# First layer's experts by slots: routed tiles of 128 rows in place of all eight experts over every row

## The reference, cut to what matters

```
x = x + tanh(g_xattn[0]) * _L0_xattn_ref(ctx_2048, _layernorm(x, axis=-1), L0_xattn_b, itok)
x = x + tanh(g_ffn[0]) * _L0_ffn_ref(_layernorm(x, axis=-1), W_qkv, b_qkv, W_gate, b_gate, W_experts, b_experts)
...
def _L0_ffn_ref(x, ...):                       # E = 8 experts, D = 256, TOP_K = 2, 16 heads of 16
    ...                                        # self-attention: attn_out
    gate = jax.nn.softmax(x @ W_gate + b_gate, axis=-1)
    top_g, top_i = jax.lax.top_k(gate, TOP_K)
    combine = jnp.sum(jax.nn.one_hot(top_i, E, dtype=x.dtype) * top_g[..., None], axis=2)
    expert_out = jnp.einsum('bsd,edf->bsef', x, W_experts) + b_experts
    moe_out = jnp.einsum('bsef,bse->bsf', expert_out, combine)
    return attn_out + moe_out
```

## Time and profile before

| | |
|---|---|
| Time, median of 3 runs | 2596.88 us (2596.45 to 2602.02) |
| The profiled execution | 2595.37 us, its span 2593.6 us |
| Busy share of the span | PE 88%, PEld 61%, DVE 64%, ACT 52%, POOL 39% |
| Unit 0's jobs | to about 385 us of the span |
| Unit 1's jobs (with the dense experts) | about 385 to 985 us |
| Units 2 and 3 | about 985 to 1520, and to 1890 us |
| Routing, second layer's experts, their sum | about 1890 to 2594 us |

### The profile page before, as it was taken

One profiled execution on the slowest core, in us unless ns is written; L12 is line 12 of the kernel. 1 busy time (PEld: TensorE's weight loads), 2 busy tenths in 40 slices (PEclk: granted clock), 3 DMA queues, 4 the chain that ended last, 5 costly groups with the idle time before them and its releaser, 6 DMA issues. The chain is left out here.

```text
span 2593.6 us, 51898 instructions
## 1 busy us (share of the span) xinstructions
PE 2280.5 (88%) x17492; PEld 1577.5 (61%) x17493; DVE 1658.5 (64%) x4377; ACT 1358.8 (52%) x2398; POOL 1004.2 (39%) x1875
## 2 busy tenths in 40 slices
PE   2889999899999999999999999999837999999950
PEld 1444555555455556666666666766527999999950
DVE  4878886677766667777767777786644434343437
ACT  3889863555336456777777788776601222222212
POOL 5556412213022135333323347887611333333323
PEclk9999998999999999999999999999956999999985
DMA  7878623314134245555555445555264111111125
GB/s 219 208 187 205 159 72 82 76 46 114 44 90 96 64 98 134 123 119 121 127 129 123 119 103 123 137 125 131 54 217 147 34 36 34 36 35 34 36 84 194
DMA packets 212014, 279.68 MB, mean 108 GB/s; under 512 B 32734, under 2 KB 156617, under 8 KB 205546
## 3 DMA queue, kind: packets, MB, share of 16 engines
q1 hardware_dynamic: 198378, 246.57, 38.5%
q0 software_dynamic: 6912, 17.97, 2.2%
q10 hardware_dynamic: 6528, 12.58, 1.3%
HBM read 193.12 MB, written 84.83 MB: 107 GB/s over the span
## 5 line engine op out<-in xcount | busy, mean ns | idle before, releaser
L1012 ACT ACTIVATE ex<-t_ps 128x512 f32<-128x512 f32 (+1 forms) x1280 | 684.9, 579 | 200.8 <-PE t_ps L918 153.8
L1163 DVE TENSOR_REDUCE mx<-s_ps 128x2 f32<-128x512 f32 (+1 forms) x1024 | 660.0, 683 | 198.4 <-PE s_ps L889 123.8
L918 PE MATMUL t_ps<-qs,ks 123*128 123x256 bf16 x2048 | 354.8, 276 | 9.6 <-ACT ex L1012 4.6
L941 PE MATMUL pv_ps<-ex,va 128*17 128x256 f32 (+1 forms) x5120 | 318.3, 375 | 0.7 <-POOL ex L1064 0.5
L1006 ACT ACTIVATE qs<-tr_ps 27x2048 bf16<-27x2048 bf16 x128 | 239.2, 1869 | 107.8 <-PE tr_ps L902 104.9
L918 PEld LDWEIGHTS t_ps<-qs,ks 123*128 123x128 bf16 x2048 | 176.4, 98 | 156.2 <-ACT ex L1012 68.3
L1571 PEld LDWEIGHTS x_up_ps<-x_rows_t,x_wnow 128*128 128x128 f32 x2272 | 267.3, 193 | 5.3 <-issue 0.9
L859 PE MATMUL pre_ps<-wexp,xt 128*128 128x512 f32 x512 | 266.3, 625 | 3.7 <-DVE moe L1225 2.7
L1571 PE MATMUL x_up_ps<-x_rows_t,x_wnow 128*128 128x128 f32 x2272 | 267.9, 277 | 1.1 <-ACT x_rows_t L1601 1.1
L1601 ACT ACTIVATE x_rows_t<-x_rt_ps 128x256 f32<-128x256 f32 x72 | 27.6, 383 | 448.5 <-PE x_rt_ps L1560 448.5
L1581 PE MATMUL x_y_ps<-wdn,x_act 128*128 x1136 | 257.1, 379 | 0.7 <-DVE x_y L1642 0.7
(11 more groups left out here) (244 smaller groups left out, 3741.4 us busy)
## 6 DMA issues: line engine op xcount, KB each, us to landing
q_parts<-pq SPq DMA_DIRECT2D x128, 192.0 KB
qs<-q_parts SPq DMA_DIRECT2D x64, 384.0 KB, 4.9
qs<-q_parts SPq DMA_DIRECT2D x192, 128.0 KB, 5.8
k_parts<-pk SPq DMA_DIRECT2D x96, 192.0 KB
ks<-k_parts SPq DMA_DIRECT2D x96, 192.0 KB
ks<-k_parts SPq DMA_DIRECT2D x288, 64.0 KB
ks<-ctx_k_parts SPq DMA_DIRECT2D x64, 192.0 KB
ks<-ctx_k_parts SPq DMA_DIRECT2D x192, 64.0 KB
```

The source lines that it names most:

```text
L918: last = pe.matmul(dst[:, t * T:(t + 1) * T], key[0:ROWS, h, t * P:(t + 1) * P], qs[q_at][0:ROWS, h, :], start=True, stop=True)
L941: last = pe.matmul(pv_ps[i * VS:i * VS + VW, q0:T], val[:, t, k * QH + i, :], e, start=r == 0 and t == 0, stop=r == srcs - 1 and t == NT - ...
L1012: act.activation(ex[:, n % EXPS, 0:w], t_ps[n % 2][:, 0:w], ACT.Exp).then_inc(t_read, 1)
L1163: dve.tensor_reduce(dst, s_ps[n % S_BANKS][:, :].rearrange("p (a b) -> p a b", a=dst.shape[-1]), AX.X, ALU.max).then_inc(s_read, 1)
```

## The change

The dense steps (`GATE`, `GEXP`, `TOP`, `CT`, `MBIAS`, `EXPERT`) and `moe` go. Instead:

- **Unit 0's jobs**, after `FIN`, also do the norm for unit 1: `HNS` (DVE), `HNP` (POOL), `HNX` (DVE, into `o`), store it (`STOREN`, 256 KB), turn it (`HT`: PE, ACT) and compute the gate's logits (`HG`: PE, DVE).
- **Unit 1's jobs** load that norm (`LOADN`) straight into `xn` in place of `LNS`, `LNP`, `LNX`.
- **The routing** of all 4096 rows is one chain, begun when the last `HG` of unit 0 is done: 23 steps `RC` on DVE, one `RX` on ACT, `RANK` on PE, then 16 chunks `RH` (DVE), `TH` (DVE, POOL), `NAME` (PE, DVE). It stands in the order between the first two jobs of unit 1.
- **71 tiles** of 128 rows, eight to each job (1, 2) to (1, 10): `XR` (POOL: indirect gather into one of 6 buffers), `XTT` (PE reads the tile's expert into a register and turns the rows; ACT copies), `XE` (PE: bias by a bf16 matmul and two f32 matmuls of 256 columns; DVE copies), `XS` (POOL: indirect scatter from one of 4 buffers). All 71 are done whatever the rows' experts are.
- **Unit 2's jobs** load the two rows per token (`LOADY`, 512 KB) and add them to x (`MOE`, four multiply-adds on DVE) before `LNS`. `LOADY` of the first job waits for all scatters.
- The second layer's `w1` and `wo` lie in the space of `wexp` and are loaded behind `LOADX` of job (3, 0), no longer at the start; the experts' bias is loaded three times at the start, behind the large weights, and cut into bf16 parts there by 10 DVE operations.

```
-    "GATE": [("pe", 0.9), ("dve", 0.65)], "GEXP": [("act", 0.22)], "TOP": [("dve", 0.6)],
-    "CT": [("pe", 0.25), ("act", 0.36)], "MBIAS": [("pe", 1.1), ("dve", 0.69)], "EXPERT": [("pe", 0.87), ("pe", 0.87), ("dve", 0.97)],
...
+def tile_job(n):
+    return 1, 2 + n // 8
...
-    s = add("LNS", 0, x, past("LNX", 2))
-    s = add("LNX", 0, add("LNP", 0, s), past("XT", 2) if u < 3 else None)
+    if u == 1:
+        s = add("LOADN", 0, ("STOREN", 0, b, 0), past("XT", 2))
+    else:
+        if u == 2:
+            y = add("LOADY", 0, *([("MOE", u, b - 2, 0)] if b >= 2 else [("XS", *tile_job(n), n) for n in range(SLOT_TILES)]))
+            x = add("MOE", 0, x, y)
+        s = add("LNS", 0, x, past("LNX", 2, 0, (0, 2, 3)))
+        s = add("LNX", 0, add("LNP", 0, s), past("XT", 2) if u < 3 else None)
...
-    if u == 1:
-        chain = add("GEXP", 0, add("GATE", 0, turned, ("FIN", u, b - 2, 0) if b >= 2 else None))
-        for n in range(TOPS):
-            chain = add("TOP", n, chain)
-        chain = add("MBIAS", 0, add("CT", 0, chain))
-        experts = [add("EXPERT", (t, e), chain) for t in range(NT) for e in range(0, E, 2)]
...
+    if u in (0, 3):
+        s = add("HNX", 0, add("HNP", 0, add("HNS", 0, s, ("HNX", u, b - 2, 0) if b >= 2 else None)))
+        if u == 0:
+            add("STOREN", 0, s)
+            s = add("HT", 0, s, past("HG", NQ))
...
+def expert_steps():
...
+    add(rc(0), *[("HG", 0, b, 0) for b in range(B)])
+    add(("RX", 1, 0, 0), rc(0))
+    for k in range(1, CHAIN):
+        after = {1: ("RX", 1, 0, 0), 9: ("RANK", 1, 0, 0), CHAIN - 2: ("NAME", 1, 0, CHUNKS - 1)}.get(k)
+        add(rc(k), rc(k - 1), after)
+    add(("RANK", 1, 0, 0), rc(7))
...
+    for n in range(SLOT_TILES):
+        add(of("XR", n), rc(CHAIN - 1), of("XTT", n - NER))
+        add(of("XTT", n), of("XR", n), of("XE", n - 2))
+        add(of("XE", n), of("XTT", n), of("XS", n - NY))
+        add(of("XS", n), of("XE", n))
...
-                sp.dma_start(bexp[:, :], a["b0_exp"]).then_inc(small_loaded, 16)
...
-                sp.dma_start(w1[:, :, :], chunked(a["w1_qkv"])).then_inc(w_loaded, 16)
-                sp.dma_start(wo[:, :, :], chunked(a["w1_o"])).then_inc(w_loaded, 16)
+                for n in range(3):
+                    sp.dma_start(bexp[n * E:(n + 1) * E, :], a["b0_exp"]).then_inc(small_loaded, 16)
...
+                    elif name == "XTT":
+                        if k == 0:
+                            pe.wait_ge(tables_ready, 1)
+                        chosen[k] = pe.value_load(expert_of[0:1, k:k + 1], min_val=0, max_val=E - 1)
+                        begin_pre(step)
+                        pe.wait_ge(er_loaded[k % NER], 16 * (k // NER + 1))
+                        for c in range(DC):
+                            last = pe.transpose(bank[:, c * P:(c + 1) * P], er[k % NER][:, c * P:(c + 1) * P], ident[:, :])
                         end_pre(step, last)
...
+                    elif name == "XE":
+                        wait_copied(pe, ("XTT", u, b, k))
+                        x = chosen.pop(k)
+                        pe.matmul(bank[:, 0:D], tile_is[:, k:k + 1].broadcast_to([3 * E, P]), bexp_parts[:, :], start=True, stop=False)
+                        for c in range(DC):
+                            last = pe.matmul(bank[:, 0:D], ert[k % 2][:, c, :], wexp[:, c, bass.ds(x, 1), :].rearrange("p e n -> p (e n)"),
+                                             start=False, stop=c == DC - 1)
+                        end_pre(step, last)
...
+                        if k >= NER:
+                            wait_turned(pool, ("XTT", *tile_job(k - NER), k - NER))
+                        pool.indirect_dma_start(er[k % NER], None, n1_d.rearrange("b p t n -> (b p t) n"),
+                                                bass.IndirectOffsetOnAxis(ap=row_of[:, k:k + 1].bitcast(U32), axis=0)).then_inc(er_loaded[k % NER], 16)
+                    elif name == "XS":
+                        wait_copied(pool, ("XE", u, b, k))
...
+                        for m in range(TOPK):
+                            for t in range(NT):
+                                last = dve.scalar_tensor_tensor(out=xs[x_at][:, t, :], in0=yb[b % 2][:, t * TOPK + m, :], scalar=first_share[:, b * NT + t, m:m + 1],
+                                                                in1=xs[x_at][:, t, :], op0=ALU.mult, op1=ALU.add)
```

More of the change, by code:

```diff
@@ L209, in job_steps @@
     if u < 2:
-        add("FIN", 0, *outs, *(experts if u == 1 else []))
+        s = add("FIN", 0, *outs)
     else:
@@ L395, in wait_stored, with rows_stored @@
     eng.wait_ge(stored[JOB[job] % NX], 16 * (JOB[job] // NX + 1))
+def rows_stored(b):
+    at = JOB[(0, b)] % NO
+    return sum(JOBS[j][0] == 0 for j in range(at, JOB[(0, b)] + 1, NO)), at
 def joint_stored(u, b):
@@ L826, in _ @@
                         bank = bank_of(step)
-                        if turn == 0:
+                        if turn == 0 and name != "XTT":
                             begin_pre(step)
```

458 lines of the change are left out of this document (332 added, 126 removed).

## The result

The changed kernel took 2581.1 us (median of seven runs, 2575.4 to 2586.6) beside 2599.4 us of the kernel before: ratio 0.9928, 95% interval 0.9914 to 0.9941. That is 18 us less where 120 were forecast, and outside the range. Measured again twice beside the experiments, the same source took 2551.2 and 2554.1 us: ratios 0.9827 (0.9809 to 0.9844) and 0.9822 (0.9803 to 0.9842), 45 us less. So some 28 us of the 102 that I missed belong to that one measurement, and some 74 us to my sum; by either the time lies outside the range. I call the trace of the first measurement "after" and the first of the two others "after, measured again"; the experiments are held against 0.9825.

The account below looks back on a forecast made before the run. PE was taken to bound units 1 and 2, with four resources nearly full in unit 0. From 2595 us, -160 + 7 + 24 + 4.5 + 5 = -119.5 gave 2476, as a median 2477; range 2435 to 2530.

Parts of the forecast that it names:

- Dense experts off PE, 266 us: Unit 1: removing dense experts, bias, gate and weight turns saves PE 16.6 us a job, 266 us for 16 jobs.
- the rival by which they had only filled PE's holes: Unit 1 is held by its own chains, so removing dense work gives little: 2560 to 2595 us; chance 0.03.
- The length of unit 1 before, 631 us: Unit 1 of the kernel before: 39.5 us a job by the rate of FIN, 631 us for the unit.
- The routing pair, 66 us: Unit 1's first two jobs, which carry the routing: about 66 us, set by DVE, against 59 on PE.
- A tile, 1.30 us of PE: Unit 1: each tile's turns and products cost PE 1.52 us, scaled 1.30, so 71 tiles cost 92 us.
- The scaling by 0.85: Unit 1: PE group times multiplied by 512/602 = 0.85, since matmuls overlap, before they count for the stage.
- The register read, 7 us: Unit 1, before each XTT: PE's read of the tile's expert costs 0.1 us, 7 us in all.
- The last five jobs, 105 us: Unit 1's five later jobs without tiles: 21 us each, 105 us together, with ACT as next limit.
- Unit 0 and the start, 28.5 us: Unit 0's added DVE work costs 1.5 us a job, 24 us; the later bias delays the start by 4.5 us.
- Unit 2, 5 us: Unit 2: MOE's four multiply-adds, 0.48 us each on DVE, cost between 0 and 31 us, taken as 5.
- POOL's issues: Unit 1's jobs with tiles: each indirect DMA issue waits for one more DVE instruction, 45 us, 2522 us; chance 0.05.
- stalls in the tile chain: Unit 1: tiles' ACT and DVE copies stand behind other work and hold PE, 43 us, 2520 us; chance 0.20.

Follow-up runs that it names:

- experiment 10: Changed kernel without the routing and without the 71 tiles, with a constant share in the addition of rows: 2383.3 us, 0.9172 of the kernel before.
- experiment 2: Changed kernel without the 71 tiles; routing, stores of normed rows and weighted addition stay: 2434.6 us, 0.9385 of the kernel before.
- experiment 13: The kernel of experiment 2 (no tiles), also without the naming steps RH, TH and NAME: 2401.8 us, 0.9242 of the kernel before.
- experiment 15: The kernel of experiment 6 with routing given to unit 1's third job, tiles over jobs four to twelve: 2506.6 us, 0.9640 of the kernel before.
- experiment 1: Changed kernel with a fixed expert for each tile, no register read or run-time weight slice, same order: 2540.5 us, 0.9781 of the kernel before.
- experiment 11: Changed kernel with unit 0's added moments and norm on 8 columns in place of 256, same order: 2553.9 us, 0.9823 of the kernel before.
- experiment 16: Changed kernel with each store of the normed x in unit 0 made twice: 2552.2 us, 0.9809 of the kernel before.
- experiment 17: Changed kernel with planner's PE costs in unit 0 raised, turns 0.44 to 0.65, logits 0.45 to 1.1 us: 2571.2 us, 0.9901 of the kernel before.
- experiment 6: Changed kernel with the addition of expert rows in four steps of one multiply-add, not one of four: 2517.2 us, 0.9692 of the kernel before.
- experiment 4: Changed kernel with the 64 multiply-adds of expert rows cut from 256 columns to 8, same order: 2537.9 us, 0.9770 of the kernel before.
- experiment 3: Changed kernel with the tiles' PE, ACT and DVE work, but only six gathers and no scatter: 2555.3 us, 0.9840 of the kernel before.

## Why the prediction was wrong, step by step

The numbers are of after, measured again, where nothing else is said. Most of what the prediction named as its signs came, unit 0 at 19.6 us a job (19.4 forecast), PE 94% busy among tiles, 21.6 us a job after them, the first load at 29.1 us; the one that failed by far is the pair with the routing, at 93.5 us in place of 66.

- **Dense experts off PE, 266 us.** Right in kind: unit 1 of the kernel before less that of experiment 10 is 266, and the rival by which they had only filled PE's holes is out. That the number agrees to the microsecond is luck: by `FIN`'s rate a job fell from 39.5 us to 20.7, by 18.8 and not 16.6, while the first job's `FIN` came 37.7 us behind unit 0 instead of 22.4.
- **The length of unit 1 before, 631 us.** Wrong by 17. It was 614.5. I took 16 times the rate of `FIN`; but the first job's `FIN` comes 22.4 us after unit 0's last (383.0 after 360.6), since its work was done inside unit 0 (its first write of `moe` is at 323.9 us). The sum credited a saving on 17 us that were never there. The working names the row; what it lacks is the end of the unit before, at 360.6 us and not near 385, where unit 1's first `FIN` stands.
- **The routing pair, 66 us.** Wrong by 27, the largest error: 93.5 us (398.3 to 491.8). The step that failed is that the pair takes DVE's time, its routing work added to its own, with PE's work fitting beside it. It did not fit. PE stood 22 of the 93 us, 17 of them for maxima, since DVE has one fixed line in which the routing stands ahead of them; DVE was busy 78 us, 12 more than my 66, and in the other 15 it waited itself, 7 of them for PE's name products. The clock's part is the smaller one: from 442 to 460 us it was 0.66, by my estimate at most 6 us of PE's time (0.34 of 18).

  The price is wrong by more than the pair shows. Unit 1 took 404 us in experiment 2 (397.9 to 801.7) and 348 in experiment 10, so the routing costs 56 us where my sum had 20; 37 of them are the naming by experiment 13. Only 30 of the 56 lie in the pair, which takes 63.6 us even without routing; the other 26 come in the jobs behind it, for which less has been done ahead. I costed the naming at 13 us on PE, where its records were busy 18.6, and on DVE only by a window of the second layer, where the same work had nothing beside it. Here every routing step carries the first job's number, by which the planner prefers it to later jobs' maxima. With it two jobs later, and the tiles with it (experiment 15), the kernel gains 14 us: so a part is order. How the rest divides between DVE's time, PE's and the order is open.
- **A tile, 1.30 us of PE.** Mis-sized: 1.6 us with its read, measured by leaving all out (experiment 2), against 1.4; 115 us for all in place of 99. The scaling by 0.85 was taken from a mix in which half was one long matmul group. In the tiles' stretch:

```profile
L1022 PE MATMUL pre_ps<-wexp,work 128*128 x284 | 81.8, 411 | 0.0
...
L1015 PE MATMUL pre_ps<-ident,work 128*128 128x128 f32 x142 | 29.2, 290 | 9.4 <-issue 5.4 <-DVE work L1408 2.2 <-ACT pq L1157 0.6
...
L1020 PE MATMUL pre_ps<-bexp_parts,tile_is 24*128 24x256 bf16 x71 | 19.9, 281 | 1.8 <-ACT pk L1157 1.7
```

  130.9 us over 71 tiles are 1.84 us each, against my unscaled 1.52: turns 0.21 in place of 0.16 us each, the bf16 record 0.28 in place of 0.18. A bf16 record lasts 281 to 283 ns in both places, but the 438 scores stood several in a row and overlapped, 78.8 us in all, and the tile's stand alone. Nine jobs with tiles took 317 us (491.8 to 809.2) against 307 with the reads: the rate was nearly right, 35.3 us a job.
- **The register read, 7 us.** 11 us by experiment 1's ratio, to some 6, and 8 by its trace. The row of the same kind was the right bound.
- **The last five jobs, 105 us.** 108 (809.2 to 917.2). Right.
- **Unit 0 and the start, 28.5 us.** 38 (398.3 against 360.6). The first load went out at 29.1 us against a forecast of 28.7, the first `FIN` at 103.9 against 96.3, and from there a job took 19.6 us against 17.6, where I had added 1.5. The reason given for it was wrong: neither DVE's work (experiment 11) nor the store (experiment 16). In the window of unit 0 every engine is less busy than before; below it the group of the logits on DVE in that window:

```profile
110.00:330.00 220.00, 188.09 (x1766) 108.92 (x1766) 170.26 (x406) 177.18 (x297) 108.53 (x213) 0.96 0.76 186
```

```profile
L1473 DVE TENSOR_TENSOR first_logits<-pre_ps,bg 128x16 f32<-128x16 f32 x12 | 2.1, 175 | 10.5 <-PE pre_ps L957 10.5
```

  DVE stands 0.9 us a job before the logits. With the planner's cost corrected (experiment 17) unit 0 ended 4 us sooner, but DVE still waited 9.8 us for the logits in that window, so that run does not price the wait. What lengthens a job of unit 0 is open.
- **Unit 2, 5 us.** 14 in unit 2 (its last `PROJ` is at 1517.1, 599.9 us from unit 1's end at 917.2, against 585.5 us before), inside my bounds, but by luck: from the first to the last `PROJ` it is 558.0 us against 523.5, 34 more and above my upper bound of 31, and 20 come back because the first one follows unit 1 sooner. Four steps (experiment 6) take the 34 away. The clock has a part in it, 0.96 in the window against 1.00 in four steps, by my estimate at most 12 us of 310. The 0.48 us of an addition were taken from an operation that reads PSUM; with both inputs in SBUF and POOL beside it, it took up to 1.43, and 0.96 in the mean of the 36 above. The Trainium skill, "SBUF — State Buffer", "Who interferes with whom", says that a DVE instruction with two SBUF inputs contends with a GpSimd instruction that reads SBUF, and that one engine then blocks for the other's whole instruction. The trace agrees (experiment 4: 0.21 to 1.31 us for 8 columns), and so do the maxima, which read PSUM and stay at 0.68. I had looked for this rule at the indirect DMAs, where it changed nothing (experiment 3), and not at `MOE`.
- **POOL's issues and stalls in the tile chain.** Neither: a scatter took 1.02 us and a gather 0.99, and without them nothing was gained (experiment 3). PE was 94% busy among tiles and stood 9.4 us before L1015 and 1.8 before L1020, 0.16 us a tile where stalls would have shown as over 0.5.

Sum of the errors, stretch by stretch: 17 (unit 1 before), 27 (the pair), 10 (the nine jobs with tiles), 3 (the last five), 9 (unit 0 and the start) and 9 (unit 2); unrounded 76 us, less 3 after unit 2, which is the 73 between the forecast's 119.5 and the 46.4 by which the two spans differ (2593.6 and 2547.2). By prices, the 41 us of unit 1 (519 against 478) are 36 for the routing and 16 for the tiles, less 9 for jobs without either (348 against 357) and 2 of rounding. The other 28 us of the result on record lie in the tiles' stretch of one measurement and stay open. Of my cases only one, that the dense work had merely filled, has a time that fits the first measurement (2560 to 2595; not the two others), and its mechanism is the one that experiment 10 excludes: a fitting time was no proof. The forecast came from a sum of eight steps, each with a bound, and six of the errors had one sign.

## What to carry to other kernels

Measure a stage from the end of the stage before it, not by its rate times its jobs: work of a stage that runs ahead is already paid. The other way round, a stage that looks cheap by its length may only have begun earlier, so look at its rate as well (unit 2: 14 us by length, 34 by rate). Price work that is put into a full line by the line's own order, since a fixed order lets it stand before what others wait for; the cheapest fixes here were to cut a long step into pieces (35 us) and to give the routing a later place (14). Where a planner makes the order, a change of one or two costs by 0.2 to 0.65 us made this kernel 20 us slower, and a set of such changes 47, so a result of that size says little of its reason; and a control measured beside the experiments is worth its run, as 28 us of one source showed.
